# One exponential of the keys: kept through DRAM from the projection, instead of a second product in the mix

## The reference, cut to what matters

```python
def softmax_kernel(data, proj, is_query):
    data_normalizer = d ** (-0.25)
    data_dash = einsum('bhnd,md->bhnm', data_normalizer * data, proj)
    diag = sum(data * data, axis=-1, keepdims=True) * 0.5 * data_normalizer ** 2
    if is_query:
        m = max(data_dash, axis=-1, keepdims=True)
    else:
        m = max(data_dash, axis=(-3, -2, -1), keepdims=True)   # over all heads, rows and features
    return ratio * (exp(data_dash - diag - m) + EPS)
...
q_prime = softmax_kernel(q, proj_mat, is_query=True)
k_prime = softmax_kernel(k, proj_mat, is_query=False)
context = einsum('bhnm,bhnd->bhmd', k_prime, v)
out = einsum('bhnm,bhmd,bhn->bhnd', q_prime, context, d_inv)
```

## Time and profile before

| | |
|---|---|
| median of three runs | 1726.52 us (1725.98 to 1729.97) |
| the profiled execution | 1718.87 us, its span 1717.1 us |
| PE busy | 1565.3 us (91%) |
| PEld | 1192.4 us (69%) |
| DVE | 1129.8 us (66%) |
| ACT | 681.6 us (40%) |
| POOL | 410.1 us (24%) |
| moved by DMA | 213.66 MB, mean 124 GB/s |

### The profile page before, as it was taken

One profiled execution on the slowest core, in us unless ns is written; L12 is line 12 of the kernel. 1 busy time (PEld: TensorE's weight loads), 2 busy tenths in 40 slices (PEclk: granted clock), 3 DMA queues, 4 the chain that ended last, 5 costly groups with the idle time before them and its releaser, 6 DMA issues.

```text
span 1717.1 us, 24932 instructions
## 1 busy us (share of the span) xinstructions
PE 1565.3 (91%) x9666; PEld 1192.4 (69%) x9731; DVE 1129.8 (66%) x2573; ACT 681.6 (40%) x1359; POOL 410.1 (24%) x251
## 2 busy tenths in 40 slices
PE   3979999999989789999999979999999999986987
PEld 2556666555655467888888868888888966656664
DVE  6677664114466978797878789767975643885223
ACT  3421001122233467777777754434643431441110
POOL 3788888888400000000000000000000000002331
PEclk9999999999999979999999999999999999996999
DMA  9335545454652223234233044334530133645941
GB/s 353 84 67 118 119 78 118 68 94 65 191 183 87 91 78 135 72 99 131 63 101 95 27 153 134 129 129 151 164 125 29 60 114 135 231 180 211 321 146 50
DMA packets 194504, 213.66 MB, mean 124 GB/s; under 512 B 80975, under 2 KB 149213, under 8 KB 194386
## 3 DMA queue, kind: packets, MB, share of 16 engines
q1 hardware_dynamic: 117762, 187.01, 33.0%
q0 software_dynamic: 75760, 22.70, 8.4%
q10 hardware_dynamic: 864, 2.36, 0.4%
HBM read 144.74 MB, written 68.40 MB: 124 GB/s over the span
## 4 chain that ended last, share of the span: by engine, by line
PE 72%; DVE 17%; ACT 4%; issue 3%; DMA 2%; SPq 1%; POOLq 0%; POOL 0%; ACTq 0%; DVEq 0%
PE bank L1047 19%; PE bank L892 12%; PE bank L893 12%; PE bank L891 12%; PE bank L1217 4%; DVE junk L1452 3%; PE bank L1205 3%; PE bank L1101 3%; PE bank L1073 2%; DVE eb L1498 1%; DVE eb L1489 1%; PE bank L1116 1%; DVE q_max L1521 1%; PE bank L1086 1%; PE bank L993 1%
## 5 line engine op out<-in xcount | busy, mean ns | idle before, releaser
L1047 PE MATMUL bank<-hb,eb 128*128 128x193 f32 (+3 forms) x2400 | 419.9, 332 | 24.7 <-DVE eb L1498 14.0
L1047 PEld LDWEIGHTS bank<-hb,eb 128*128 128x128 f32 (+3 forms) x2400 | 400.3, 190 | 38.3 <-DVE eb L1498 17.1
L2093 POOL DMA_INDIRECT table<-amount,place x170 | 345.1, 2030 | 71.5 <-issue 49.5
L2099 POOL IOTA iota8i<- 128x8 int32 x1 | 0.1, 139 | 934.6 <-DMA node_rows<-node 934.6
L1489 DVE SCALAR_TENSOR_TENSOR eb<-shift_b,as_low,shift_b 128x640 f32<-128x640 f32 (+1 forms) x240 | 196.3, 859 | 7.8 <-DMA shift_b<-shift_rows 7.8
L1882 ACT ACTIVATE eb<-eb,asd 128x640 f32<-128x640 f32 (+1 forms) x240 | 182.0, 814 | 45.9 <-DVE eb L1489 45.9
L1498 DVE SCALAR_TENSOR_TENSOR eb<-eb,count 128x1280 f32<-128x1280 f32 (+1 forms) x120 | 174.4, 1454 | 12.4 <-ACT eb L1882 12.4
L1452 DVE CUSTOM_DVE_ANT_0 junk<-ab,absent 128x1250 bf16<-128x1250 f32 x120 | 174.4, 1453 | 1.0
L891 PE MATMUL bank<-wg_hi,x1T_hi 128*128 128x384 bf16 (+3 forms) x360 | 117.9, 328 | 0.6 <-DVE x1T_lo L1319 0.6
L893 PE MATMUL bank<-wg_hi,x1T_lo 128*128 128x384 bf16 (+3 forms) x360 | 117.9, 327 | 0.0
L892 PE MATMUL bank<-wg_lo,x1T_hi 128*128 128x384 bf16 (+3 forms) x360 | 117.8, 327 | 0.0
(11 more groups left out here) (288 smaller groups left out, 2944.1 us busy)
## 6 DMA issues: line engine op xcount, KB each, us to landing
w<-in_w SPq DMA_DIRECT2D x16, 1152.0 KB, 20.1
shift_b<-shift_rows SPq DMA_DIRECT2D x24, 625.0 KB, 5.9
h_rows<-h_row SPq DMA_DIRECT2D x27, 388.0 KB
hb<-h_rows SPq DMA_DIRECT2D x12, 873.0 KB
ar<-node_rows SPq DMA_DIRECT2D x27, 384.0 KB
table<-zero POOLq DMA_DIRECT2D x3, 3054.0 KB, 21.1
tab<-table SPq DMA_DIRECT2D x27, 312.5 KB, 3.4
qk_rows<-qk_row SPq DMA_DIRECT2D x12, 625.0 KB
```

The lines of the kernel that those rows point to most:

```text
L1047: ins = T.matmul(bank[w // 2][0:M, c0:c0 + GC + 1], p[0:K, u, w * P:w * P + M], hv[0:K, t, 0:GC + 1], start=opens and u == 0 and w % 2 == ...
L2093: G.indirect_dma_start(tables[i], bass.IndirectOffsetOnAxis(place[:, c:c + 1], axis=0), amount16[:, c:c + 1], None, compute_op=ALU.add).th ...
```

## The change

- The products come in the order of all six k, then all six q. `k_top` of pair n - 1 runs beside product n = 1 to 6, and PE's wait for a free bank becomes a wait for k_kept.
- Each top is kept: DVE takes the maximum and its negative, ACT writes exp(top - row maximum) to one of three buffers e_out (`k_keep`), SP stores it to e_rows in DRAM (60 tiles of 256 KB).
- `top_max`, `top_turn` and `top_spread` run beside q's products 23 to 25; k_shift gets the row maxima added, and ACT takes its exponential once: a factor for each row and head.
- In the mix k has no dash and no exponential. `k_feat` is two Relus of 256 columns, in place, with that factor as scale and eps as bias. The ten tiles of pair 0 are loaded in `pair_in` 0, now at m = 21; the others by `e_load`, four places of the mix's order ahead, into a ring of five. kT and its loads go.
- Counts begin at m = 16, `count_turn` and `absent` are one step further behind (lag 3), early edge maxima run at 1.0 a tick and those of layers 1 and 2 at 0.8; edge attention also waits until the mix is at its place 21.

Worked out from these rates: the mix stands at ticks 145 to 284, `shifts` 0 at 167, `edge_z` 0 at 172, `gather` 0 at 178, the last `edge_max` near 270, and 16 instead of 13 edge maxima stand before the mix.

```diff
+AHEAD, RING, LOOK = NT, 5, 4
...
-COUNTS_AT = 17
-COUNT_RATE, EARLY_EDGE_RATE, FIRST_EDGE_RATE, EDGE_RATE, ATTENTION_RATE = 0.5, 0.75, 1.1, 0.6, 0.5
+COUNTS_AT = 16
+COUNT_RATE, EARLY_EDGE_RATE, FIRST_EDGE_RATE, EDGE_RATE, ATTENTION_RATE = 0.5, 1.0, 1.1, 0.8, 0.5
...
-            if n % 2 and 2 * c + part:
+            yield from (("k_keep", i) for i in unkept)
+            unkept.clear()
+            if 1 <= n <= PAIRS and 2 * c + part:
...
-                    yield "k_top", NT * (n // 2) + t
+                    yield "k_top", NT * (n - 1) + t
+                    unkept.append(NT * (n - 1) + t)
...
-        if m == NC * 4:
+        if m == NC * (PAIRS + 1):
...
+        for i, name in enumerate(("top_max", "top_turn", "top_spread")):
+            if m == NC * (PAIRS + 1) + i:
+                yield name, 0
...
-    yield "top_max", 0
-    yield None
-    yield "top_turn", 0
-    yield None
-    yield "top_spread", 0
...
-    yield from paced((in_step([(2, lambda t: [("count_turn", t), ("absent", t)]), (1, lambda t: [("count", t)]),
+    yield from paced((in_step([(3, lambda t: [("count_turn", t), ("absent", t)]), (1, lambda t: [("count", t)]),
...
-    yield None
-    yield None
+    while "first" not in done:
+        yield None
...
+        if n == 2 * NT + 1:
+            done.add("first")
...
-        if kind:
-            yield "dash", pair, kind, t
+        if n + LOOK < len(order):
+            next_pair, next_kind, next_t = order[n + LOOK]
+            if next_pair and next_kind == "k":
+                yield "e_load", NT * next_pair + next_t
+        if kind == "q":
+            yield "dash", pair, t
...
-        def keys_of(pair):
-            return kT[pair % 2] if pair else k_first
+        def kept_of(n):
+            return e_first[n] if n < AHEAD else ek[(n - AHEAD) % RING]
+        def kept_in(n):
+            i = n - AHEAD
+            return ("e_first_in", 16 * AHEAD) if i < 0 else (f"e_in{i % RING}", 16 * (i // RING + 1))
+        def used(n, kind):
+            return dash_of(n // NT, kind, n % NT) + 1
...
-                pe.wait_ge("qk_lo", NC * (2 * pair + 1))
-                pe.wait_ge("k_max", i - 1)
-                dash_into(4 + i % 2, qk_out[0], t).then_inc(sem["top_mm"], 1)
+                pe.wait_ge("qk_lo", NC * (pair + 1))
+                pe.wait_ge("k_kept", i - 1)
+                dash_into(4 + i % 2, qk_out[pair % 2], t).then_inc(sem["top_mm"], 1)
...
+                pe.wait_ge("k_kept", PAIRS * NT)
...
-            def dash(pair, kind, t):
-                g = dash_of(pair, kind, t)
-                if g == 0:
-                    pe.wait_ge("k_max", PAIRS * NT)
+            def dash(pair, t):
+                q = NT * pair + t
+                if q == 0:
+                    pe.wait_ge("k_kept", PAIRS * NT)
...
-                pe.wait_ge(f"{kind}_in{pair % 2}", 16 * (pair // 2 + 1))
-                pe.wait_ge("mix_exp", g - 1)
-                dash_into(3 + g % 2, (keys_of if kind == "k" else queries_of)(pair), t).then_inc(sem["dash_mm"], 1)
+                pe.wait_ge(f"q_in{pair % 2}", 16 * (pair // 2 + 1))
+                pe.wait_ge("mix_exp", q - 1)
+                dash_into(3 + q % 2, queries_of(pair), t).then_inc(sem["dash_mm"], 1)
...
-                g = dash_of(pair, "k", t)
+                n = NT * pair + t
...
-                pe.wait_ge("k_feat", NT * pair + t + 1)
+                pe.wait_ge("k_feat", n + 1)
...
-                        ins = T.matmul(cv[:, m, hh, :], ef[g % 4][0:R, hh, m * 128:(m + 1) * 128],
+                        ins = T.matmul(cv[:, m, hh, :], kept_of(n)[0:R, hh, m * 128:(m + 1) * 128],
...
-                g = dash_of(pair, "q", t)
...
-                pe.wait_ge("mix_exp", g + 1)
+                pe.wait_ge("mix_exp", q + 1)
...
-                                      ef[g % 4][0:R, hh, m * 128:(m + 1) * 128], ident_of(t))
+                                      ef[q % 4][0:R, hh, m * 128:(m + 1) * 128], ident_of(t))
...
+                ve.wait_ge("k_max", 2 * i + 1)
+                V.tensor_scalar(kneg[0:R, i:i + 1], kmax[0:R, i:i + 1], -1.0, None, ALU.mult).then_inc(sem["k_max"], 1)
...
-                ve.wait_ge("k_max", PAIRS * NT)
+                ve.wait_ge("k_max", 2 * PAIRS * NT)
...
-                ve.wait_ge("diag_in", 2 * PAIRS * NC)
+                ve.wait_ge("diag_in", PAIRS * NC)
...
+                ve.wait_ge("top_v", 4)
+                ks = k_shift[:, :, :].rearrange("p t (a h) -> p t a h", h=2)
+                V.tensor_tensor(ks, ks, kmax[:, :].rearrange("p (a t) -> p t a", t=NT).unsqueeze(3).broadcast_to(
+                    [P, NT, PAIRS, 2]), ALU.add).then_inc(sem["top_v"], 1)
...
-            def exps(pair, kind, t):
-                R = rows(t)
-                g = dash_of(pair, kind, t)
-                se.wait_ge("top_v", 4)
-                if kind == "k":
-                    se.wait_ge("dash_mm", g + 1)
-                else:
-                    se.wait_ge("q_max", 2 * (NT * pair + t) + 2)
-                se.wait_ge("feat_used", g - 3)
+            def k_keep(i):
+                R = rows(i % NT)
+                if i < 3:
+                    se.wait_ge(f"h_out{i}", 16 * (NT * LAYERS // 3))
+                se.wait_ge(f"e_out{i % 3}", 16 * (i // 3))
+                se.wait_ge("k_max", 2 * i + 2)
+                A.activation(e_out[i % 3][0:R, :], bank[4 + i % 2][0:R, :], ACT.Exp,
+                             bias=kneg[0:R, i:i + 1]).then_inc(sem["k_kept"], 1)
+            def top_spread(_):
+                se.wait_ge("top_v", 5)
+                A.activation(k_shift[:, :, :], k_shift[:, :, :], ACT.Exp).then_inc(sem["k_scale"], 1)
+            def k_feat(pair, t):
+                R = rows(t)
+                n = NT * pair + t
+                e = kept_of(n)
+                se.wait_ge("k_scale", 1)
+                se.wait_ge(*kept_in(n))
...
-                    bias = (k_shift[0:R, t, 2 * pair + hh:2 * pair + hh + 1] if kind == "k"
-                            else q_shift[0:R, t, hh:hh + 1])
-                    ins = A.activation(ef[g % 4][0:R, hh, :], bank[3 + g % 2][0:R, hh * FEATS:(hh + 1) * FEATS],
-                                       ACT.Exp, bias=bias)
+                    ins = A.activation(e[0:R, hh, :], e[0:R, hh, :], ACT.Relu, bias=eps[0:R, :],
+                                       scale=k_shift[0:R, t, 2 * pair + hh:2 * pair + hh + 1])
+                ins.then_inc(sem["k_feat"], 1)
+            def q_exp(pair, t):
+                R = rows(t)
+                q = NT * pair + t
+                se.wait_ge("top_v", 5)
+                se.wait_ge("q_max", 2 * q + 2)
+                if q >= 4:
+                    se.wait_ge("feat_used", used(q - 4, "q"))
+                for hh in range(2):
+                    ins = A.activation(ef[q % 4][0:R, hh, :], bank[3 + q % 2][0:R, hh * FEATS:(hh + 1) * FEATS],
+                                       ACT.Exp, bias=q_shift[0:R, t, hh:hh + 1])
...
-            def k_exp(pair, t):
-                exps(pair, "k", t)
-                g = dash_of(pair, "k", t)
-                e = ef[g % 4][0:rows(t), :, :]
-                se.wait_ge("mix_exp", g + 1)
-                A.activation(e, e, ACT.Relu, bias=eps[0:rows(t), :]).then_inc(sem["k_feat"], 1)
-            def q_exp(pair, t):
-                exps(pair, "q", t)
...
+            def k_keep(i):
+                pair, t = divmod(i, NT)
+                sy.wait_ge("k_kept", i + 1)
+                S.dma_start(e_rows[pair, at(t), :], e_out[i % 3][0:rows(t), :]).then_inc(sem[f"e_out{i % 3}"], 16)
+            def load_kept(n):
+                pair, t = divmod(n, NT)
+                sy.wait_ge(f"e_out{n % 3}", 16 * (n // 3 + 1))
+                S.dma_start(kept_of(n)[0:rows(t), :, :].rearrange("p h m -> p (h m)"),
+                            e_rows[pair, at(t), :]).then_inc(sem[kept_in(n)[0]], 16)
+            def e_load(n):
+                sy.wait_ge("qk_mm", NC * 2 * PAIRS)
+                if n >= AHEAD + RING:
+                    sy.wait_ge("feat_used", used(n - RING, "k"))
+                load_kept(n)
...
-                    sy.wait_ge(f"qk_out{j}", 16 * (PAIRS if pair else 1))
+                    sy.wait_ge(f"qk_out{j}", 16 * (PAIRS if pair else PAIRS // 2 + 1 - j))
...
+                if pair == 0:
+                    for n in range(AHEAD):
+                        load_kept(n)
...
-                    sy.wait_ge("dash_mm", dash_of(pair - 2, "k", NT - 1) + 1)
-                    sy.wait_ge("feat_used", dash_of(pair - 2, "k", NT - 1) + 1)
-                S.dma_start(keys_of(pair)[:, :, :], qk_rows[1, pair]).then_inc(sem[f"k_in{i}"], 16)
+                    sy.wait_ge("feat_used", used(NT * (pair - 2) + NT - 1, "k"))
...
-                    sy.wait_ge("dash_mm", dash_of(pair - 2, "q", NT - 1) + 1)
+                    sy.wait_ge("dash_mm", NT * (pair - 1))
```

55 lines of the change are left out of this document (35 added, 20 removed), and 4 rows, old and new, of the table TAKEN_OVER.

## The result

The changed kernel takes 1734.84 us (median of 5 runs, 1733.63 to 1739.21) against 1726.52 us of the kernel before: a ratio of 1.0052, 95% interval 1.0037 to 1.0067. It is slower by half a per cent, where the forecast was 1702.0 with a range of 1684 to 1731. The size was missed by 33 us, and the sign with it.

What follows compares the result with a forecast made beforehand. PE was taken to bound most of the mix, with DVE 17% below as the next bound. Terms +3 - 2 - 10 - 6.5 - 9 = -24.5 us took the profiled 1718.9 to 1694.4, or 1702.0 as median; range 1684 to 1731.

Steps and rivals of the forecast that it cites:

- Step 1: Projection and edge maxima of layer 0: kept exponentials and the new order together cost +3 us, between -8 and +15.
- Stores: I take 0: Projection: the 60 stores of 256 KB, issued by SP from three buffers, cost no time.
- Ten loads: nothing: Projection: pair 0's ten loads, issued during q's products and needed 40 us later, cost no time.
- Step 2: From the shifts to the first gather: -2 us, so the first gather stands at 661 against 660.
- over 25 us: Sign of being wrong: PE's clock at 0.5 before the first gather for over 25 us.
- Step 3: Mix beside gathers: 72.5 us a pair with PE and DVE equally full, 333 us for 106 ticks, -10 us.
- rival (a): Mix: DVE does not hold PE up, a pair takes 70.4 us, total 1686 us; chance 0.17.
- k_feat waiting for a load of e: Sign of being wrong: in the mix, k_feat waits for a load of e; no size given.
- Step 4: Gathers done by the end of the mix: 53 instead of 51, each 3.27 us, saving 6.5 us later on.
- Step 5: Behind the mix, 1003 to 1052 us: no edge maxima left among weight splits, -9 us (0 to -12).
- Rival (c): Projection: round trip of top, max, exponential and store costs 1.6 us per pair of tops, +48, total 1750 us; chance 0.15.
- Rival (d): Projection: ACT reloads its function table at each change from square to exponential, some +30, total 1732 us; chance 0.03.

Runs made afterwards that it cites:

- order_only: Kernel before with the changed kernel's order of products, counts and maxima and its rates, but no kept exponential and k's second product still in the mix: 1719.8 us, ratio 0.9957.
- pair_late: Changed kernel with pair 0's ten loads of e issued after the 30th chunk of products instead of the 21st: 1727.4 us, ratio 1.0012.
- warm: Changed kernel plus an unused product of the size of a dash behind each sum of keys of pairs 0 and 1: 1733.2 us, ratio 1.0038.

## Why the prediction was wrong, point by point

The forecast and the trace of after in the same cuts: products 206.5 and 223.3 us, to the first gather 81.5 and 81.7, to the weights 342 and 358.2, to the end 690 and 697.9. With the first product 3.4 us late that is 45 us between 1692.6 and the span of 1737.5; 12 of it is the scale (before's profiled execution was 7.6 us under its median, after's 4.4 over).

- **Step 1, projection and edge maxima of layer 0, +3: this is the step that failed.** It cost +23, and order_only, without the keeping, +4. In the step's own terms (us from the start of the span):

  | | forecast | order_only | after |
  |---|---|---|---|
  | first count begins | 481 | 477.8 | 486.4 |
  | last count begins | 547.7 | 541.1 | 565.7 |
  | shifts of layer 0 | 634 | 635.9 | 654.7 |

  The forecast's +12 for the end of the products had order and keeping in it. Order_only measured 9, after 32, so the keeping's share, which was to be some 4 us of waits and what it adds to four turns of the counts, was 22 (223.3 - 201.2), 19 of it idle time of PE. By product, against order_only: 4.8 us in products 1 to 4, 13.0 in 5 and 6 where counts meet tops, 6.2 in 8, and -1.9 in the rest. Term by term: the start of the counts (5.4 us late, 3.4 of it with the first product) and the first four turns (40.6 us for 37.6) were near, but not for the reasons given. The waits in narrow chunks were 0.24 to 1.42 us for 0.2 to 0.3, and "Stores: I take 0" was 5.0 us over products 1 to 5, 3.23 of them one wait of PE behind one store. The five later turns took 38.7 us for 29.1. "Ten loads: nothing" was 6 us of that (the turns take 32.9 in pair_late); I had read the DMA share and the due time, but of what stood behind them in SP's queue I named only the w_loads and left out the tables. And of the 13.0 us in products 5 and 6, 7.5 are there with a short exponential and small stores too: single waits of 3 to 4 us. I had added the exponential's own length to the loop, but not its place in ACT's queue behind a count copy that waits for DVE, nor the place of its maximum on DVE. PE's clock had no term in this step: 30.7 us at half speed in the products, 6.8 before.
- **Step 2, first gather, -2: right**, 26.6 us behind the shifts for 27 worked out (28.5 before). The clock fell as its bound allowed (61.2 us at half speed between the last product and the first gather, 29.0 before; "over 25 us" stood among the signs of being wrong), and the 0 that I took for it was right (warm). The profile's reading was: DVE leads there, so the clock of PE costs nothing. The Trainium skill (TensorE: Matmul & The Clock Gate, Part 1) has half rate as the default and activity as what lifts it; the fall agrees with that, and no time came of it.
- **Step 3, -10, at 72.5 us a pair: mechanism right, one term missing.** The stage took 6.1 us more than before instead of 10 less (358.2 us; 352.1 before). From the last query maximum of pair 1 to that of pair 5 it was 73.9 us a pair (before 75.2, order_only 76.2), with 19.0 us of waits for loads of e in the stage. With POOL's loads it was 70.7, which is rival (a)'s 70.4, and the stage took 345.2 us for the 342 of the forecast. DVE does not hold PE up much, and the waits for loads and the lower clock behind them took back 3.2 of the 5.5 us a pair that were there to be had (76.2 - 70.7). "k_feat waiting for a load of e" stood among the signs, but had no place in the sum.
- **Step 4, two more gathers done by the end of the mix:** 57 instead of 55 have begun when the weights start. Right in number; for its 6.5 us see the next step.
- **Step 5, -9 behind the mix:** right from 1003 to 1052 (45.8 of 49 us, 93% busy). But steps 4 and 5 together were 15.5 us and measured 7.2 (705.1 to 697.9), and order_only has them too (698.4). Lost again was up to 7.3 us at the last gather: "from 1052 PE leads and nothing of its work changes" was true of the work and not of the order. That the end of the gathers moved against the row blocks is the likely reason, since the wait goes from none before to 4.81 us with the new rates alone; no run shows it by itself.
- **Rival (c)**, the round trip, has the mechanism that made the kernel slower, at less than its price: 22 us in the products, less the ten loads' 6, is 0.5 us for each of 30 pairs of tops, below the 1.0 from which it said that it decides. It decided all the same, since the loads in the queue and the mix's waits came on top. It was kept too small by taking one mechanism at a time. That its price came near (1750 against 1734.8) is in part luck: the waits that it prices came to a third of its 48 us, and the rest came from the loads, the mix and the stretch behind it. Its chance of 0.15 was too low.
- **Rival (d)** fell. The trace has one load of the table in the projection and none at a change from Square to Exp:

```profile
392.98 1.28 ACT L1954 ACT_TABLE_LOAD   x1 [0.52 <-DVE kneg L1441]
394.27 1.26 ACT L1954 ACTIVATE e_out<-bank,kneg 128x512 f32<-128x512 f32 x2
396.85 1.48 ACT L1954 ACTIVATE e_out<-bank,kneg 128x512 f32<-128x512 f32 x2 [1.31 <-DVE kneg L1441]
398.46 0.60 ACT L1901 ACTIVATE sq<-bank 128x512 f32<-128x512 f32 x1
```

  The rule of the Trainium skill that cheap functions are in every set (ScalarE: Activation LUTs, Table sets: the hidden batching unit) agrees with it, though it names relu, copy, identity and abs there and not the square; the trace shows it for the square.

What stays open: how the 5.5 us that product 6 keeps with the early place divide among the late table, the late maximum and the clock, what the half clock in the products and the mix costs by itself, and why late counts help with keeping and harm without it.

## What to carry to other kernels

Work that moves from a full engine to an idle one is not free when it frees a buffer: its price is its place in that engine's queue, and what the instruction ahead of it waits for, more than its own length. A DMA is judged first by what is issued right behind it on the same queue (here a table, 7.5 us later, for which DVE waited 5.92 us), and only then by when its data are due. And when a change has an order and a trade in it, time the order alone first: here it was the part that gained.

## What the runs showed of the hardware

One execution differs from the next by up to some 8 us in the same instructions (220.9 to 228.0 us for the products in five kernels, with 27.3 to 41.0 us of them at half clock), so stages of two profiles are compared beside a third. An exponential of 8 columns took 0.27 us and one of 512 columns 0.69; shortening 60 of them by 0.42 us, 25 us of ACT, gave 3.1 us over five products in which they freed a bank. With 39 us of matmuls fewer in PE's list and more waits, PE was at half clock for 182 us instead of 93, and its busy time was only 5.5 us shorter. PE's clock rose from 0.70 to 0.87 for products done for nothing, and no time came of it.
